# Cross-attention and FFN on one core: the prologue in another order, loads over both queues, scores ahead of VW

## The chip, the cores and the metric

One core of a Trainium2 chip runs the whole program. The metric is the device time of one execution in microseconds (us). TensorE is called PE, VectorE DVE, ScalarE ACT, GpSimd POOL and SyncE SP, as in the profile.

## The reference, cut to what matters

x is 2 x 1024 x 256, the context 2 x 77 x 192, all fp32.

```python
x = x + xattn(layernorm(x), ctx, Wq, Wk, Wv, Wo, bo)   # 8 heads of 64
x = x + ffn(layernorm(x), gamma, beta, ...)
# xattn: softmax((h @ Wq) (ctx @ Wk)^T * 64**-0.5) @ (ctx @ Wv) @ Wo + bo
# ffn:   h = layernorm(x) * gamma + beta; w = (q - 128) * scales (fc1: 256 x 1024, fc2: 1024 x 256)
#        x + 0.5 * (silu(h @ w1 + b1) @ w2 + b2)
```

## The kernel before

**What is computed.** x is worked on in eight pairs (a = 0 to 7) of two tiles of 128 rows; pairs 0 to 3 are batch 0, 4 to 7 batch 1. Since the context is short, keys and queries are folded once for each batch b: M = Wq K^T (256 x 616, called M{b}.{n}: n // 2 is the half of the 256 rows, n % 2 the even or the odd heads) and VW = V Wo (616 x 256, VW{b}.0 to .2). For a pair the work is then: transposes of x (XT), scores (S{a}.{j}: x M), the maximum over each head subtracted (DVE), exp with the row's rstd as scale (ACT), sums and reciprocals (DVE), normalize (POOL), transposes of the probabilities (PT), attention_out (AO: probabilities times VW, with bo as one more row of VW), the second layer norm (hn), its transposes (HT), fc1 in four parts (F1.{a}.{p}), silu (ACT), fc2 (F2.{a}.{j}), the sum and the store. Every matmul operand in fp32 is split into a high and a low part, and three products are added: the high part is a copy by ACT (DVE for h), the low part a subtraction, by DVE for x, M, VW, probabilities, h and w2, by POOL for w1 and y.

**What sets the order.** Nothing is scheduled: each engine's block is a list of calls, and that list is the order in which it works. Engines wait for each other by semaphores. PSUM is six buffers (S0 and S1 of two banks, H0, H1, T0, T1 of one). The list `order` (line 62) says which result takes which buffer after which: a result can be written when its predecessor in the same buffer has been freed, and each buffer counts how often it was filled and freed.

**The places that the change touches.** SP's and ACT's blocks begin with the loads (lines 223 to 235, 353 to 358); SP then waits until VW0.2 is free and writes bo's two halves into the bias rows (238 to 241), and only behind that issues q2, s2 and the x pairs 3 to 7 (242 to 245); the bias rows of batch 1 follow when VW1.2 is free. POOL (323 to 349): rsqrt1 (rstd of the first layer norm, which exp needs), dequantize_w1, normalize, lower_w1, rsqrt2 (the roots of the second one: one for each tile that hn needs, then the residual's), lower_y, add_b2. DVE from 638, ACT from 445, PE from 856. On PE, `scores` waits for all four parts of M where a % 4 = 0 (796), `attention_out` for VW and the bias rows of its batch (816 to 819), again only where a % 4 = 0. From pair 2 on each engine runs a loop (499, 692, 916; POOL from pair 1, 337).

Of the kernel before, what the change touches and what calls it, by code (L numbers as in the profile page):

```python
# [13 lines left out]
P = 128  # L14
# [11 lines left out]
def build_program(nc, x, ctx_in, wq, wk, wv, wo, bo, gamma, beta, q1, s1, b1, q2, s2, b2, out):  # L26
# [39 lines left out]
    for a in range(1, NA):  # L66
        if a > 1:
            order += [(f"S{a}.0", "S0"), (f"S{a}.1", "S1"), (f"F2.{a - 2}.1", "T1"), (f"HT{a - 1}", "S0")]
        order += [(f"F1.{a - 1}.{p}", f"H{1 - p % 2}") for p in range(HP)]
        order += [(f"PT{a}.0", "S1"), (f"PT{a}.1", "S0"), (f"AO{a}.0", "T0"), (f"AO{a}.1", "T1")]  # L70
        order += [(f"XT{a + 1}", "S1")] * (a < LAST) + [(f"F2.{a - 1}.0", "T0")]
# [8 lines left out]
    with ExitStack() as stack:  # L80
# [45 lines left out]
        table_probe = small("table_probe", [P, 1])  # L126
# [66 lines left out]
        bo_hi_done, bo_split = sem("bo_hi_done"), sem("bo_split")  # L193
# [25 lines left out]
        with nc.Block() as block:  # L219

            @block.sync
            def _(sp):
                sp.dma_start(ctx_sb[:, :, :], ctx_v).then_inc(ctx_in_sem, 16)
                sp.dma_start(wq_sb[:, :, :], wq.rearrange("(n p) f -> p n f", p=P)).then_inc(wq_in, 16)
# [33 lines left out]
            def _(pool):  # L258
# [54 lines left out]
                def dequantize_w1(n):  # L313
                    c, cols = n // 2, slice(n % 2 * F // 2, (n % 2 + 1) * F // 2)
# [3 lines left out]
                def lower_w1(n):  # L318
                    c, cols = n // 2, slice(n % 2 * F // 2, (n % 2 + 1) * F // 2)
# [5 lines left out]
                nc.gpsimd.tensor_scalar(b2_half[:, :], b2_half[:, :], 0.5, None, ALU.mult).then_inc(b2_done, 1)  # L325
                pool.wait_ge(s1_in, 16 * C)
                for n in range(2 * C - 1):
                    dequantize_w1(n)
                normalize(0, 0)
                normalize(0, 1)  # L330
                dequantize_w1(2 * C - 1)
                for n in range(2 * C):
                    lower_w1(n)
                rsqrt1(1)
                rsqrt2(0)
                pool.wait_ge(b2_done, 1)
                for a in range(1, NA):
# [6 lines left out]
                    rsqrt2(a)  # L344
# [7 lines left out]
            def _(act):  # L352
                act.dma_start(wk_sb[:, :, :], wk.rearrange("(n p) f -> p n f", p=CC)).then_inc(wk_in, 16)
                act.dma_start(x_sb[:, pair(0), :], x_v[:, pair(0), :]).then_inc(x_in[0], 16)
                act.wait_ge(half_ready, 1)
                nc.scalar.activation(table_probe[:, :], neg_half[:, 0:1], ACT.Exp)
# [78 lines left out]

                def shift_w1(n):
                    c, cols = n // 2, slice(n % 2 * F // 2, (n % 2 + 1) * F // 2)
                    nc.scalar.activation(w1_sb[:, c, cols], q1_sb[:, c, cols], ACT.Copy, bias=-ZERO_POINT).then_inc(w1_shifted, 1)

                def split_w1(n):  # L440
                    c, cols = n // 2, slice(n % 2 * F // 2, (n % 2 + 1) * F // 2)
# [48 lines left out]
                for n in range(2):  # L490
                    half = slice(n * M // 2, (n + 1) * M // 2)
                    act.wait_ge(w2_done, n + 1)
                    nc.scalar.activation(w2_hi[:, half, :], w2_sb[:, half, :], ACT.Copy).then_inc(w2_hi_done, 1)
# [484 lines left out]
```

## Time and profile before

| | |
|---|---|
| three runs, median (lowest, highest) | 189.31 us (188.37, 191.15) |
| the profiled execution | 188.6 us |
| its span, first to last instruction | 186.8 us |
| busy share of the span: PE, DVE, ACT, POOL | 97%, 66%, 66%, 62% |
| granted clock of PE, mean | 0.998 |
| DMA | 10.72 MB, mostly in the first 28 us |

The page has a line of tenths for each engine (40 slices of 4.7 us). PE is at 9 from about slice 11 to the end but for the last; DVE has its fullest stretch, 9 or close to it, in slices 4 to 11 (14 to 51 us), which is the prologue. Ends of matmuls are modelled and overlap the next one, so where PE waits is read from the distances between starts, not from its busy time.

### The profile page before, as it was taken

What the parts mean: (1) busy time and instruction counts of PE and PEld (TensorE: products, weight loads), DVE (VectorE), ACT (ScalarE), POOL (GpSimd) and SP (SyncE); (2) the same over time, 40 slices, a digit from 0 to 9 for tenths busy, and PEclk for the clock granted to TensorE, in tenths of its full rate; (3) what the DMA queues carried; (4) which work ended last, traced back from release to release, by engine and by line L of the source; (5) the groups of instructions that cost most, each with busy time, mean ns of one, the idle gap of its engine ahead of it and who ended that gap; (6) DMA issues with size and microseconds to landing.
All of it is one profiled execution on the core that took longest, in us unless ns stands there. A gap on an engine that the chain in (4) does not pass through costs nothing.

```text
span 186.8 us, 3886 instructions
## 1 busy us (share of the span) xinstructions
PE 180.7 (97%) x1502; PEld 177.0 (95%) x1502; DVE 122.4 (66%) x261; ACT 122.5 (66%) x230; POOL 116.2 (62%) x159
## 2 busy tenths in 40 slices
PE   7999899899899999999999999999999999999994
PEld 7999699689899999999999999999999999999994
DVE  0287988899969464964496557937594768255341
ACT  3287880599918981898368944896289817962580
POOL 5032998569983977099707972597439762776220
PEclk9999999999999999999999999999999999999999
DMA  6997990000000100010001000100001000100101
GB/s 171 325 399 185 357 353 13 2 0 4 2 0 0 60 0 0 4 56 0 4 0 56 4 0 0 33 30 0 0 4 56 0 4 0 56 4 0 56 4 56
DMA packets 9480, 10.72 MB, mean 57 GB/s; under 512 B 2268, under 2 KB 8183, under 8 KB 9335
## 3 DMA queue, kind: packets, MB, share of 16 engines
q1 hardware_dynamic: 8837, 9.70, 15.7%
q10 hardware_dynamic: 626, 0.79, 1.5%
q8 instruction: 12, 0.20, 0.4%
q14 instruction: 5, 0.04, 0.1%
HBM read 8.38 MB, written 2.10 MB: 56 GB/s over the span
## 4 chain that ended last, share of the span: by engine, by line
PE 78%; DVE 9%; POOL 9%; ACT 1%; issue 1%
PE T L852 22%; PE H L838 21%; PE T L823 11%; PE S L802 11%; PE S L809 4%; PE S L755 3%; POOL q_sb L316 3%; POOL w_lo L321 3%; PE S L733 2%; DVE w_lo L631 2%; POOL probs L279 1%; DVE q_sb L625 1%; PE T L740 1%; PE H L740 1%; POOL rstd L290 1%
## 5 line engine op out<-in xcount | busy, mean ns | idle before, releaser
L311 POOL TENSOR_TENSOR y_lo<-y,y_hi 128x512 fp32r<-128x512 f32 x28 | 37.6, 1363 | 2.1 <-ACT y_hi L434 1.6
L279 POOL TENSOR_TENSOR probs<-probs,rsum 128x616 f32<-128x616 f32 x16 | 19.1, 1218 | 31.4 <-DVE rsum L583 31.4
L852 PE MATMUL T<-w_hi,y_hi 128*128 128x256 f32 x128 | 36.7, 286 | 0.6 <-DVE x_sb L594 0.6
L838 PE MATMUL H<-hT_hi,w_hi 128*128 128x256 f32 x128 | 36.7, 287 | 0.1
L838 PE MATMUL H<-hT_lo,w_hi 128*128 128x256 f32 x128 | 35.5, 277 | 0.0
L838 PE MATMUL H<-hT_hi,w_lo 128*128 128x256 f32 x128 | 35.5, 277 | 0.0
L852 PE MATMUL T<-w_lo,y_hi 128*128 128x256 f32 x128 | 35.5, 277 | 0.0
L852 PE MATMUL T<-w_hi,y_lo 128*128 128x256 f32 x128 | 35.4, 277 | 0.0
L430 ACT ACTIVATE y<-H,vec 128x256 f32<-128x256 f32 x64 | 26.5, 467 | 6.6 <-PE H L838 6.6
L403 ACT ACTIVATE probs<-probs,rstd 128x616 f32<-128x616 f32 x16 | 12.9, 807 | 27.1 <-DVE probs L571 27.1
L588 DVE TENSOR_TENSOR pT_lo<-S,pT_hi 128x640 fp32r<-128x640 f32 x16 | 13.1, 823 | 18.1 <-ACT pT_hi L407 18.1
L852 PEld LDWEIGHTS T<-w_hi,y_hi 128*128 128x128 f32 x128 | 24.1, 188 | 0.9 <-DVE x_sb L594 0.9
L838 PEld LDWEIGHTS H<-hT_hi,w_hi 128*128 128x128 f32 x128 | 24.1, 188 | 0.5 <-issue 0.5
L852 PEld LDWEIGHTS T<-w_lo,y_hi 128*128 128x128 f32 x128 | 24.1, 189 | 0.0
L838 PEld LDWEIGHTS H<-hT_lo,w_hi 128*128 128x128 f32 x128 | 24.1, 188 | 0.0
L852 PEld LDWEIGHTS T<-w_hi,y_lo 128*128 128x128 f32 x128 | 24.1, 188 | 0.0
L838 PEld LDWEIGHTS H<-hT_hi,w_lo 128*128 128x128 f32 x128 | 24.1, 188 | 0.0
L823 PE MATMUL T<-vw_hi,pT_hi 128*128 128x256 f32 x80 | 22.4, 280 | 0.0
L823 PE MATMUL T<-vw_lo,pT_hi 128*128 128x256 f32 x80 | 22.1, 277 | 0.0
L823 PE MATMUL T<-vw_hi,pT_lo 128*128 128x256 f32 x80 | 22.1, 277 | 0.0
L434 ACT ACTIVATE y_hi<-y 128x512 fp32r<-128x512 f32 x32 | 20.2, 632 | 1.0
L564 DVE TENSOR_REDUCE smax<-S 128x8 f32<-128x616 f32 x16 | 12.8, 799 | 12.0 <-PE S L802 11.5
(127 smaller groups left out, 460.6 us busy)
## 6 DMA issues: line engine op xcount, KB each, us to landing
q_sb<-in_L_ffn_fc_q SPq DMA_DIRECT2D x2, 1024.0 KB, 8.0
out_x<-x_sb SPq DMA_DIRECT2D x16, 128.0 KB, 1.8
x_sb<-in_x SPq DMA_DIRECT2D x7, 256.0 KB, 8.2
s_sb<-in_L_ffn_fc_scales SPq DMA_DIRECT2D x2, 512.0 KB, 12.0
s_sb<-in_L_ffn_fc_scales SPq DMA_DIRECT2D x1, 1024.0 KB, 7.7
wq_sb<-in_L_xattn_Wq SPq DMA_DIRECT2D x1, 512.0 KB, 5.6
wo_sb<-in_L_xattn_Wo SPq DMA_DIRECT2D x1, 512.0 KB, 8.1
wk_sb<-in_L_xattn_Wk ACTq DMA_DIRECT2D x1, 384.0 KB, 4.1
```

The source lines that it names most:

```text
L279: nc.gpsimd.tensor_tensor(p, p, rsum[:, j, :].unsqueeze(2).to_broadcast([P, HEADS, J]), ALU.mult).then_inc(norm_done, 1)
L311: nc.gpsimd.tensor_tensor(y_lo[:, two, :], y[:, two, :], f32(y_hi[:, two, :]), ALU.subtract).then_inc(y_lo_done, 1)
L403: nc.scalar.activation(probs[:, j, 0:HJ], probs[:, j, 0:HJ], ACT.Exp, scale=rstd1[:, t:t + 1]).then_inc(exp_done, 1)
L430: ins = nc.scalar.activation(y[:, m, :], r[:, q * W:(q + 1) * W], ACT.Silu, bias=b1_sb[:, m:m + 1])
L434: nc.scalar.activation(y_hi[:, two, :], y[:, two, :], ACT.Copy).then_inc(y_hi_done, 1)
L564: nc.vector.tensor_reduce(smax[:, j, :].rearrange("p (n h) -> p n h", n=2), s, AX_X, ALU.max).then_inc(max_done, 1)
L588: nc.vector.tensor_tensor(flat(pT_lo[:, j, :, :]), ps[bank][:, 0:JC * P], flat(f32(pT_hi[:, j, :, :])), ALU.subtract).then_inc(freed[bank], 1)
L802: ins = mm(o, xt[:, c, j * P:(j + 1) * P], m[:, b, c, h, 0:HALF], start=n == 0, stop=n == len(steps) - 1)
L809: ins = nc.tensor.transpose(r[:, m * P:(m + 1) * P], probs[:, j, m * P:(m + 1) * P], ident[:, :])
L823: ins = mm(r[:, 0:D], p[:, j, m, :], v[:, b * JC + m, :], start=n == 0, stop=n == len(steps) - 1)
L838: ins = mm(r[:, q * W:(q + 1) * W], wt[:, c, m * P:(m + 1) * P], ht[:, c, :], start=c == q == i == 0, stop=c == q == 1 and i == 2)
L852: ins = mm(o, yt[:, m, j * P:(j + 1) * P], wt[:, m, :], start=m == 0 and i == 0, stop=m == M - 1 and i == 2)
```

## The change

- **Loads.** Wk is loaded in halves of 96 rows, one on ACT's queue, one on SP's behind ctx and ahead of Wq; `wk_in` is awaited at 32.
- **PE.** Five warm matmuls at the start instead of eight. scores(0, .) stands right behind M0, ahead of the three VW0. M1.0 stays near the first probabilities, M1.1 goes behind VW1.2, just ahead of fc1(0, 0). fc1(0, 2) goes between the two prob_transposes of pair 1, x_transposes(2) ahead of attention_out(1, .), and fc2(0, 0) behind scores(2, .).
- **Finer waits.** scores(0, 0) waits for the even parts of M before its first half, for the odd ones before its second (new semaphore m_even_done). The bias rows are awaited ahead of the last chunk of attention_out, not at its start. w1 is split by column halves first (c = n % 2), so that fc1(0, 0) and (0, 1) wait for two of four quarters, fc1(0, 2) for all.
- **POOL.** It takes over bo's split. normalize(0, .) stands behind one dequantize_w1 instead of three. rsqrt2 is split in root2 (for hn) and residual_roots; the root2 of pair 0 stand ahead of rsqrt1(1) and of the last two lower_w1. In pair 1 rsqrt1(2) stands behind two lower_y, and root2(1, .) ahead of the last.
- **ACT and DVE** follow PE's order; make_hn(0) is parted around score_maxima(1, 0); the w2_hi parts and lower_w2 are parted, and lower_w2(1) goes behind add_attention(1, 1). residual(0) goes into the first round of the loop, ahead of scale_h(1).
- **Place list.** S0.0 and S0.1 swap buffers, M1.2 and M1.3 share S0.

```diff
-             ("M0.0", "H1"), ("M0.1", "T0"), ("M0.23", "S0"), ("VW0.2", "T1"), ("VW0.0", "H0"), ("S0.0", "S0"), ("S0.1", "S1"),
+             ("M0.0", "H1"), ("M0.1", "T0"), ("M0.23", "S0"), ("S0.0", "S1"), ("S0.1", "S0"), ("VW0.2", "T1"), ("VW0.0", "H0"), ("VW0.1", "T0"),
...
+                sp.dma_start(wk_sb[:, 1, :], wk[CC:DC, :]).then_inc(wk_in, 16)
                 sp.dma_start(wq_sb[:, :, :], wq.rearrange("(n p) f -> p n f", p=P)).then_inc(wq_in, 16)
...
-                act.dma_start(wk_sb[:, :, :], wk.rearrange("(n p) f -> p n f", p=CC)).then_inc(wk_in, 16)
+                act.dma_start(wk_sb[:, 0, :], wk[0:CC, :]).then_inc(wk_in, 16)
...
                     for h in range(2):
+                        if j == 0 and a % AB == 0:
+
+                            wait_freed(pe, m_home(b, h)[0])
+                            if h == 0:
+                                pe.wait_ge(m_even_done, b + 1)
+                            else:
+                                wait_freed(pe, m_home(b, 3)[0])
...
-                warm(8)
+                warm(5)
...
                 for c in range(C):
                     make_m(0, c)
+                scores(0, 0)
+                scores(0, 1)
                 pe.wait_ge(wo_in, 16)
...
                 make_vw(0, 2)
                 make_vw(0, 0)
-                scores(0, 0)
-                scores(0, 1)
                 make_vw(0, 1)
                 x_transposes(1)
-                make_m(1, 0)
                 pe.wait_ge(probs_ready, 1)
                 prob_transposes(0, 0)
-                make_m(1, 1)
+                make_m(1, 0)
                 prob_transposes(0, 1)
...
                 make_vw(1, 1)
                 make_vw(1, 2)
-                pe.wait_ge(w1_split, 2 * C)
+                make_m(1, 1)
                 fc1(0, 0)
                 fc1(0, 1)
                 prob_transposes(1, 0)
+                fc1(0, 2)
                 prob_transposes(1, 1)
-                fc1(0, 2)
                 fc1(0, 3)
+                x_transposes(2)
                 attention_out(1, 0)
                 attention_out(1, 1)
-                x_transposes(2)
-                fc2(0, 0)
                 for a in range(2, LAST):
                     scores(a, 0)
                     scores(a, 1)
+                    if a == 2:
+                        fc2(0, 0)
                     fc2(a - 2, 1, range(1))
```

PE behind M of batch 0, before (kT and wqT make M, wo_sb and vT VW, m and xT scores):

```order
L774 MATMUL S<-kT,wqT 128x77 x8
L786 MATMUL T<-wo_sb,vT 128x256
L786 MATMUL H<-wo_sb,vT 128x256 x3
L802 MATMUL S<-m_hi,xT_hi 128x308
L802 MATMUL S<-m_lo,xT_hi 128x308
```

and in the changed kernel:

```order
L799 MATMUL S<-kT,wqT 128x77 x8
L834 MATMUL S<-m_hi,xT_hi 128x308
L834 MATMUL S<-m_lo,xT_hi 128x308
...
L813 MATMUL T<-wo_sb,vT 128x256
L813 MATMUL H<-wo_sb,vT 128x256 x3
L813 MATMUL T<-wo_sb,vT 128x256 x4
L780 MATMUL S<-ident,x_sb 128x128 x4
L841 MATMUL S<-ident,probs 128x128 x5
```

Scores now follow M with nothing between them, and the three VW stand together behind.

POOL around the first normalize (probs<-probs,rsum), before:

```order
L316 TENSOR_TENSOR q_sb<-q_sb,s_sb 128x512 x3
L279 TENSOR_TENSOR probs<-probs,rsum 128x616 x2
L316 TENSOR_TENSOR q_sb<-q_sb,s_sb 128x512
L321 TENSOR_TENSOR w_lo<-q_sb,w_hi 128x512 x4
L272 TENSOR_SCALAR veps<-mv 128x2
L274 TENSOR_TENSOR rstd<-veps,neg_half 128x2
L287 TENSOR_SCALAR vars<-mv 128x1
L290 TENSOR_TENSOR rstd<-vars,neg_half 128x1
```

and in the changed kernel:

```order
L319 TENSOR_TENSOR q_sb<-q_sb,s_sb 128x512
L280 TENSOR_TENSOR probs<-probs,rsum 128x616 x2
L319 TENSOR_TENSOR q_sb<-q_sb,s_sb 128x512
L324 TENSOR_TENSOR w_lo<-q_sb,w_hi 128x512 x2
L319 TENSOR_TENSOR q_sb<-q_sb,s_sb 128x512 x2
L287 TENSOR_SCALAR vars<-mv 128x1
L290 TENSOR_TENSOR rstd<-vars,neg_half 128x1
```

One dequantize stands ahead of normalize, and two lower_w1 have moved behind the roots.

DVE between pair 1's reciprocals and the h of pair 1 (q_sb<-q_sb,s_sb dequantizes w2), in the changed kernel:

```order
L571 SCALAR_TENSOR_TENSOR m_lo<-S,m_hi 128x308 x2
L651 SCALAR_TENSOR_TENSOR q_sb<-q_sb,s_sb 128x1024 x2
L614 TENSOR_TENSOR pT_lo<-S,pT_hi 128x640
L579 TENSOR_TENSOR vw_lo<-T,vw_hi 128x512
...
L585 TENSOR_TENSOR xT_lo<-S,xT_hi 128x512
L657 TENSOR_TENSOR w_lo<-q_sb,w_hi 128x1024
L620 TENSOR_TENSOR x_sb<-T,x_sb 128x256
...
L657 TENSOR_TENSOR w_lo<-q_sb,w_hi 128x1024
L630 SCALAR_TENSOR_TENSOR hn<-x_sb,mv,rstd 128x256 x2
```

Before, the two vw_lo and the statistics stood ahead of the dequantization, no m_lo stood here, both lower_w2 (w_lo) stood ahead of the additions of attention (x_sb<-T,x_sb), and the low part of x pair 2 (xT_lo) behind them.

## Rows read from the trace of the kernel before

**Rows 1.** The page, engines: busy us (share of the span) xinstructions
```profile
PE 180.7 (97%) x1502; PEld 177.0 (95%) x1502; DVE 122.4 (66%) x261; ACT 122.5 (66%) x230; POOL 116.2 (62%) x159
```

**Rows 2.** Windows, core 0: stretch, its length, busy us (xinstructions), clock, DMA share, GB/s
```profile
5.80:11.40 5.60, 5.60 (x44) 5.53 (x44) 2.30 (x6) 2.84 (x7) 0.23 (x1) 1.00 1.08 343
...
0.00:58.40 58.40, 54.89 (x426) 51.66 (x427) 44.34 (x89) 37.21 (x72) 38.43 (x52) 1.00 0.45 145
58.40:187.00 128.60, 125.78 (x1078) 125.38 (x1076) 78.10 (x174) 85.31 (x159) 77.81 (x107) 1.00 0.05 18
```

**Rows 3.** Timeline of PE: start us, us, engine, line, operation [idle before <-releaser]
```profile
12.44 1.06 PE L774 MATMUL S<-kT,wqT 64*128 64x77 f32 x16
...
15.12 0.44 PE L802 MATMUL S<-m_hi,xT_hi 128*128 128x308 f32 x1
...
20.61 0.63 PE L755 MATMUL S<-ident,x_sb 128*128 128x128 f32 x4
...
22.79 0.74 PE L809 MATMUL S<-ident,probs 128*128 128x128 f32 x5 [0.51 <-issue]
...
24.51 0.77 PE L809 MATMUL S<-ident,probs 128*128 128x128 f32 x5
...
33.89 0.66 PE L755 MATMUL H<-ident,hn 128*128 128x128 f32 x4 [0.53 <-DVE hn L604]
...
34.38 2.33 PE L786 MATMUL T<-wo_sb,vT 128*128 128x256 f32 x10
...
36.84 0.36 PE L838 MATMUL H<-hT_hi,w_hi 128*128 128x256 f32 x1
...
40.94 0.77 PE L809 MATMUL S<-ident,probs 128*128 128x128 f32 x5 [0.41 <-POOL probs L279]
...
49.02 0.38 PE L852 MATMUL T<-w_hi,y_hi 128*128 128x256 f32 x1 [0.65 <-DVE x_sb L594]
```

**Rows 4.** The chain that ended last: start us, us, what
```profile
1.03 3.78 PE S L733 x16
...
21.48 2.39 POOL probs L279 x2
...
25.11 4.99 POOL w_lo L321 x4
```

**Rows 5.** By source line, L733: ns min/median/max, first and last start
```profile
L733 PE MATMUL S<-warm_sb x18: 275/422/580, 1.0 to 5.4; 128*128 128x128 f32 x18
```

**Rows 6.** DMA issues: queue, operation xcount, KB each, us from issue to landing
```profile
wq_sb<-in_L_xattn_Wq SPq DMA_DIRECT2D x1, 512.0 KB, 5.6
...
wk_sb<-in_L_xattn_Wk ACTq DMA_DIRECT2D x1, 384.0 KB, 4.1
```

**Rows 7.** Timeline of DVE, columns as in rows 3
```profile
14.01 0.86 DVE L544 SCALAR_TENSOR_TENSOR m_lo<-S,m_hi 128x308 fp32r<-128x308 f32 x2
...
17.14 0.80 DVE L564 TENSOR_REDUCE smax<-S 128x8 f32<-128x616 f32 x1 [0.36 <-PE S L802]
...
21.19 0.20 DVE L583 RECIPROCAL rsum<-ssum 128x8 f32<-128x8 f32 x1
...
39.04 0.20 DVE L583 RECIPROCAL rsum<-ssum 128x8 f32<-128x8 f32 x1
...
54.60 0.80 DVE L571 TENSOR_TENSOR probs<-S,smax 128x616 f32<-128x616 f32 x1
```

**Rows 8.** Timeline of POOL and ACT, as in rows 3; last row by source line
```profile
17.65 3.78 POOL L316 TENSOR_TENSOR q_sb<-q_sb,s_sb 128x512 f32<-128x512 f32 x3 [4.48 <-ACT q_sb L438]
...
42.50 1.55 POOL L274 TENSOR_TENSOR rstd<-veps,neg_half 128x2 f32<-128x2 f32 x1
...
62.35 0.71 POOL L274 TENSOR_TENSOR rstd<-veps,neg_half 128x2 f32<-128x2 f32 x1
...
69.53 1.08 ACT L420 ACTIVATE x_sb<-x_sb,res_shift,res_scale 128x256 f32<-128x256 f32 x2
...
L631 DVE TENSOR_TENSOR w_lo<-q_sb,w_hi x2: 1542/1927/2312, 44.9 to 46.3; 128x1024 fp32r<-128x1024 f32 x2
```

More of the change, by code:

```diff
@@ L325, in _ @@
                 nc.gpsimd.tensor_scalar(b2_half[:, :], b2_half[:, :], 0.5, None, ALU.mult).then_inc(b2_done, 1)
+                pool.wait_ge(bo_in, 16)
+                nc.gpsimd.tensor_copy(bo_hi[:, :], bo_sb[:, :]).then_inc(bo_hi_done, 1)
+                pool.wait_ge(bo_hi_done, 1)
+                nc.gpsimd.tensor_tensor(bo_lo[:, :], bo_sb[:, :], f32(bo_hi[:, :]), ALU.subtract).then_inc(bo_split, 1)
                 pool.wait_ge(s1_in, 16 * C)
-                for n in range(2 * C - 1):
-                    dequantize_w1(n)
+                dequantize_w1(0)
                 normalize(0, 0)
                 normalize(0, 1)
-                dequantize_w1(2 * C - 1)
-                for n in range(2 * C):
-                    lower_w1(n)
+                dequantize_w1(1)
+                lower_w1(0)
+                lower_w1(1)
+                dequantize_w1(2)
+                dequantize_w1(3)
+                root2(0, 0)
+                root2(0, 1)
                 rsqrt1(1)
-                rsqrt2(0)
+                lower_w1(2)
+                lower_w1(3)
+                residual_roots(0)
                 pool.wait_ge(b2_done, 1)
-                for a in range(1, NA):
+                normalize(1, 0)
+                normalize(1, 1)
+                lower_y(0, 0)
+                lower_y(0, 1)
+                rsqrt1(2)
+                lower_y(0, 2)
+                root2(1, 0)
+                root2(1, 1)
+                lower_y(0, 3)
+                residual_roots(1)
+                add_b2(0)
+                for a in range(2, NA):
                     normalize(a, 0)
@@ L488, in _ @@
                 prob_hi(1, 0)
+                vw_hi_part(1, 1)
                 prob_hi(1, 1)
[L490 to L493, printed above, removed]
+                vw_hi_part(1, 2)
+                x_hi(2)
+                w2_hi_part(0)
                 hidden(0, 2)
+                w2_hi_part(1)
                 hidden(0, 3)
[L496 to L498 removed]
+                nc.scalar.activation(table_probe[:, 0:1], neg_half[:, 0:1], ACT.Exp)
                 for a in range(2, NA):
                     exponential(a, 0)
+                    if a == 2:
+                        residual(0)
                     scale_h(a - 1)
                     exponential(a, 1)
[L503 removed]
+                    nc.scalar.activation(table_probe[:, 1:2], neg_half[:, 0:1], ACT.Silu)
                     hidden(a - 1, 0)
@@ L545, in m_lo_part @@
                                                          f32(m_heads(m_hi, b, n)), ALU.mult, ALU.subtract)
-                    if (b, n) != (0, 2):
-                        ins.then_inc(freed[bank], 1)
+                    ins.then_inc(m_even_done if n == 2 else freed[bank], 1)
                 def vw_lo_part(b, n):
@@ L684, in _ @@
                 prob_lo(1, 0)
+                vw_lo_part(1, 1)
+                stats1(2)
                 prob_lo(1, 1)
+                vw_lo_part(1, 2)
+                x_lo(2)
                 lower_w2(0)
-                lower_w2(1)
                 add_attention(1, 0)
                 add_attention(1, 1)
-                x_lo(2)
+                lower_w2(1)
                 make_hn(1)
@@ L777, in make_m, with make_vw @@
                             fill(homes[e][0], ins[e])
-                def make_vw(b, n):
-                    r = emptied(f"VW{b}.{n}")
-                    for q in range(min(2, JC - 2 * n)):
+                def make_vw(b, n, qs=range(2)):
+                    if qs[0] == 0:
+                        emptied(f"VW{b}.{n}")
+                    r = ps[place[f"VW{b}.{n}"][0]]
+                    for q in qs[:JC - 2 * n]:
                         m = 2 * n + q
```

121 lines of the change are left out of this document (59 added, 62 removed), and 4 rows, old and new, of the table order.

## The prediction

> **What bounds the kernel now.** I read the page first: TensorE (PE) is busy for 97% of the 186.8 us span [rows 1]. The windows view then splits the span. From 58.4 us on, which the change leaves as it is, PE is busy 125.8 of 128.6 us (what is missing lies at the very end, in work that is not touched); what can be removed lies in the prologue, 0 to 58.4 us [rows 2]. A busy PE there hides work that merely follows other work, so I went by the starts of PE's stages. In PE's timeline [rows 3] six stages don't start right behind the last record ahead of them: the transposes of x pair 1 (20.61), of the first probabilities (22.79), of hn (33.89), fc1 (36.84), the second probabilities of pair 1 (40.94) and fc2 (49.02). Beyond the usual 0.12 from start to start these are about 0.35, 0.65, 0.7, 0.4, 0.55 and 0.8 us, 3.5 us together. (The idle time that the rows print is counted from a modelled end and is smaller.) Who ends them: POOL, which in the chain of work holds everything from 21.48 on with normalize and the split of w1 [rows 4], then DVE with hn and x_sb [rows 3]. So at most 3.5 us, plus what the start gives, is to be had: 2% of the span. The rest is matmuls that are neither added nor removed.
>
> **The change, stage by stage.** I carry the start of each PE stage forward, each with the durations of the rows. "Now" is the kernel before.
>
> *Start.* Three warm matmuls go: six records; 16 take 3.78 us with the modelled tail of the last [rows 4], a new one each 0.21, so 1.28 us. What follows waits for ctx. When that lands the views don't say; wk, issued at the same time on the other queue, took 4.1 us, to about 4.8 [rows 6]. So the gain is between 0 and 1.28; the transposes of ctx now stand directly behind the last warm record, and I take 0.2, near the lower end. K then starts behind the two copies of ctxT, not behind wk, so halving wk over two queues earns nothing. It puts 192 KB more ahead of wq on SP's queue. wq landed at 1.20 + 5.6 = 6.8 and is wanted at 7.85 [rows 6]; at the 343 GB/s of that stretch [rows 2] 192 KB is up to 0.6 us, and x's first tiles lose as much on the other queue. It stays hidden: cost 0, 0 to 0.3 if not. M's last half (16 records from 12.44 [rows 3]) now ends at 13.4, in the new order 13.2.
>
> *Scores ahead of VW.* Eight records of VW, 1.7 us between M and scores at 15.12, are gone from there. But scores needs the low parts of M, the even one for its first half: DVE makes them from 14.01 for 0.86 us, two in a row [rows 7], so the first is there at 14.45, 14.25 with the earlier start. Scores starts at 14.35 instead of 15.12. PE idles about 1.1 us, where it had VW: this is a new wait. Then 3.4 us of scores (24 records) and 3.4 of the three VW (16 records, 0.21 each as in the ten from 34.38) bring the x transposes to 21.15 (20.61 now).
>
> *First probabilities.* The DVE chain from smax (17.14) to the end of the reciprocal (21.19 + 0.2) [rows 7] moves 0.77 earlier, to 20.6. POOL does one dequantize (1.26, of 3.78 for three, from 17.65 on) ahead of normalize, not three, and is free [rows 4, 8]; the two operations on bo that it takes over lie in its 4.48 us of idle time ahead of the dequantize and cost nothing (if not, 1.2 each at most, as one of 128x512). Normalize takes 1.2 (2.39 for two), so the transposes start at 22.0 (22.79 now); PE waits 0.4. The second pair: rsum waits for a vw_lo of 0.41, to 22.0; normalize to 23.2; x_lo, which frees the bank, to 23.3; transposes at 23.6 (24.51 now [rows 3]). One M is no longer in front of them. From there VW, attention and scores run closed for 8.7 us as now (33.9 less the wait of 0.7, less 24.5), to 32.3.
>
> *hn.* POOL's queue after normalize is re-dealt: one dequantize, two lower_w1 with a wait of about 0.65 for ACT's copy ahead of the second, two more dequantize (5 x 1.26 + 0.65 behind 23.2, to 30.15), then the roots that hn needs (0.85 each; the second wants mv at 30.2) to 31.9, hn 0.48 behind smax, to 32.7. Transposes of h at 32.8 (33.89 now), PE waits 0.5.
>
> *fc1.* VW 2.05 (ten records), and the M that was moved here, 0.95 (16 records) [rows 3]: fc1 starts at 36.4 (36.84 now). split_h would be ready at 35.7: the moved M fills the 0.4 us wait that stood here. fc1 needs only half of w1 split, 27.6. POOL ends the rest of w1 at 35.4 and the residual roots at 37.5, so normalize of pair 1 runs 37.6 to 40.0. PE: transposes 39.3, fc1 39.9, second transposes 41.3 (0.55 wait gone, because fc1(0,2) lies between), fc1 and x transposes to 43.8, attention 43.85 to 47.3. Now attention starts at 44.28 and still has the x transposes (0.45) behind it: 0.9 us ahead. Its banks are freed by vw_lo at 43.0 and 45.2; the bias rows of batch 1 are first waited for at pair 4. Those of batch 0 are issued when vw_lo ends (21.2 instead of 15.5), and q2, s2 and five x pairs are queued behind them, 5.7 us later, from about 22.7; q2 and s2, 1 MB each, are 6 us at 343 GB/s, and DVE wants them at 39, so 0.
>
> *fc2 behind scores.* The 0.8 us for which fc2(0,0) waited on DVE [rows 3] is covered by scores: scores at 47.35, fc2 50.8 to 53.6, then 3 records. Transposes of h 1 could start at 54.0 (55.59 now). DVE is next: from its last reciprocal (39.04 + 0.2) to the end of the subtraction that frees the bank (54.60 + 0.8) it takes 16.2 us, 1.5 of it the two waits for POOL's roots [rows 7]. In the new order it starts 0.75 earlier, carries two m_lo (0.86) more and has the second lower_w2 over one or both waits: 38.5 + 0.85 + 14.7 = 54.05. So 54.15. Last, residual(0) (1.08 [rows 8]) now stands in ACT ahead of scale_h(1): exp 0.8, residual 1.08, scale 0.5, split 0.75 behind 54.05 give fc1(1,0) at 57.25, against 58.43 now: 1.2 us ahead. The residual also delays DVE's ssum, so POOL's normalize(2,0) ends at about 60.1 where PE wants it at 59.97: 0.2 back.
>
> *POOL beside DVE.* While DVE dequantizes w2, POOL's small root operation takes 1.55 us at 42.50, and 0.71 at 62.35 [rows 8]. The new order puts normalize(1,1) there (39.05 on). If it is stretched alike it ends at 41.4 and PE waits 0.1; two-sided bound 0 to 1. I take 0. The Trainium skill (GPSIMD Engine Reference, Specifications) says why: POOL shares its SBUF interfaces with VectorE when that reads two SBUF inputs. The rows agree; by its rule the loss sits at this place.
>
> Sum: 0.2 (start) + 0.6 (scores earlier, 14.35 for 15.12 less the start) are what the softmax chain gets; carried through, 1.2 us at fc1(1,0), less 0.2: **1.0 us**. The profiled execution took 188.6 us (span 186.8 and 1.8 around it): 187.6. The three runs shown have 189.31 as median, 0.7 above it, and 188.37 as lowest; I add 0.2 for that: **187.8**.
>
> **Rivals.**
> (a) *Clock.* Warm records at the start take 422 ns, the last one, at 5.4, takes 275 [rows 5]. So PE starts at the lower of its levels (1.2 GHz) and gets 2.4 GHz around 5.3, after 4.3 us of matmuls almost without a pause. With five warm matmuls PE pauses from 3.2 until ctx lands, up to 1.1 us. If only the work behind the pause counts, the rise comes at 4.2 + 4.3 = 8.5: 3.1 us at half speed, a loss of 1.55, and 187.8 becomes 189.3, slower than before. It decides as soon as the rise comes over 2 us later, that is after 7.3. For it: nothing else changes in that stretch. Against it: the pause is a quarter of it at most. The Trainium skill (TensorE: Matmul & The Clock Gate, Part 1) tells that the default state is throttled and activity releases it, which is this rival's rule; this trace has no pause to try it on. 15%.
> (b) *Nothing arrives.* The 1.1 us wait for M, DVE's chain and residual(0) in ACT give back the rest; each term of 0.1 to 0.4 is as large as my error in a hand-off. 187.8 + 1.0 = 188.8. 17%.
> (c) *More arrives.* ctx is there by 3.5 (another 0.6), and hn or DVE's queue is not late (0.5 + 0.3): 187.8 - 1.4 = 186.4; all waits gone would be 188.6 - 3.5 - 0.2 = 184.9. 13%.
> (d) *DVE late.* With lower_w2 at 2.31 rather than 1.54 us each beside POOL's lower_y [rows 8], fc2's second half and hn come up to 1.5 later: 187.8 + 1.5 = 189.3. 5%.
> Forecast, a gain of 0.4 to 1.8: 50%.
>
> **Numbers.** Leaving out the far ends of (a) and (c), 185.9 to 189.5 holds 8 in 10. Faster by over 2% (about what a measurement of this kernel can tell from no change) is below 185.5: only the far end of (c) with a low draw of runs, 8%. Slower by over 2% is above 193.1, beyond every rival: 3%. Within 2%: 89%.
>
> **What would show it.** PE: ctx transposes 0.2 earlier; a gap of about 1.1 ahead of scores; probability transposes at 22.0; h transposes at 32.8; no gap at fc1, at the second transposes of pair 1 or at fc2; fc1(1,0) at 57.2. A PE record of 422 ns behind 5.8 speaks for (a). A gap ahead of the h transposes at 54, or of fc2's middle, speaks for (d). I am wrong if ctx is late, if wq is, or if hand-offs between engines (0.05 to 0.15 each in the rows) are longer in the new order.

## The result, and the profile after

The changed kernel takes 193.7 us (median of 4; 193.59 to 194.71) against 189.11 us before (4; 188.37 to 191.15): a ratio of 1.0243, with a 95% interval of 1.0188 to 1.0297. It is slower by 4.6 us, where 187.8 us was forecast, 1.3 us below this median of before, and the time lies outside the range of 185.9 to 189.5. Here and below, a ratio leaves out the few slow executions, more than 1.5% above the fastest of their kernel, while a median is of all. The profiled execution took 193.6 us, its span is 191.8 us.

The page's engine line and the first line of the chain of work that ended last (shares of the span by engine), to be read beside [rows 1]:

```profile
PE 182.9 (95%) x1496; PEld 178.5 (93%) x1496; DVE 125.1 (65%) x260; ACT 122.7 (64%) x229; POOL 117.4 (61%) x161
...
PE 78%; DVE 11%; POOL 3%; ACT 2%; DMA 2%; issue 1%
```

PE is busy 2.2 us longer (180.7 before) though it has six matmuls fewer: some of them ran slower. The rest of the 5.0 us by which the span has grown is waiting. The waits view of PE lists what it waited for (us in total, times, longest; "PE S L780 <- DVE pT_lo L614" is a transpose at line 780 into buffer S that waited for DVE's operation at line 614):

```profile
PE S L780 <- DVE pT_lo L614: 1.2, 1, 1.2
PE S L834 <- DVE m_lo L571: 1.1, 1, 1.1
PE T L899 <- DMA ctx_sb<-in_ctx: 1.1, 1, 1.1
...
PE H L874 <- DVE hT_lo L639: 0.7, 1, 0.7
PE H L780 <- DVE hn L630: 0.4, 1, 0.4
...
PE T L856 <- DVE vw_lo L579: 0.2, 1, 0.2
```

m_lo and ctx were foreseen. pT_lo (ahead of the transposes of x pair 2), hT_lo (ahead of fc1(1,0)) and vw_lo (ahead of the second half of attention) were not. The windows view, cut at the starts of M, of the first transposes of h (HT) and of fc1(1,0), first of before and then of after (columns as in [rows 2]), tells how much each stretch lost (the fourth row of after is the rest of the span):

```profile
0.00:11.49 11.49, 10.31 (x66) 9.97 (x67) 2.78 (x8) 4.69 (x10) 2.99 (x12) 1.00 0.90 275
11.49:33.89 22.40, 21.27 (x179) 19.50 (x179) 19.20 (x41) 13.38 (x28) 17.21 (x19) 1.00 0.70 235
33.89:58.43 24.54, 23.35 (x183) 22.22 (x184) 22.39 (x41) 19.17 (x34) 18.23 (x23) 1.00 0.01 1
```

```profile
0.00:14.09 14.09, 11.94 (x61) 11.26 (x61) 2.78 (x8) 4.73 (x11) 3.03 (x12) 1.00 0.85 264
14.09:35.83 21.74, 20.07 (x164) 18.63 (x163) 18.00 (x38) 12.57 (x25) 14.94 (x17) 1.00 0.63 209
35.83:63.25 27.42, 24.91 (x199) 23.17 (x199) 25.71 (x41) 19.95 (x36) 21.04 (x27) 1.00 0.03 8
63.25:191.80 128.55, 125.94 (x1076) 125.44 (x1076) 78.62 (x175) 85.44 (x159) 78.42 (x107) 1.00 0.05 18
```

The start lost 2.60 us, the stretch from M to HT gained 0.66, the one from HT to fc1(1,0) lost 2.88, of which 0.95 is M1.1, moved there out of the stretch ahead. Leaving M1.1 out, the first stretch lost 0.29 and the second 1.93. Behind 63.25 us nothing has changed (128.55 against 128.37).

**The start.** PE's timeline of after:

```profile
1.04 2.50 PE L758 MATMUL S<-warm_sb 128*128 128x128 f32 x10 [1.04 <-DVE warm_sb L664]
4.66 0.46 PE L899 MATMUL T<-ident,ctx_sb 77*96 77x77 f32 x2 [1.11 <-DMA ctx_sb<-in_ctx]
...
5.85 2.39 PE L765 MATMUL T<-ctxT,wk_sb 96*128 96x154 f32 x8
8.03 2.26 PE L765 MATMUL H<-ctxT,wk_sb 96*128 96x154 f32 x8
10.09 1.06 PE L773 MATMUL H<-ident,wq_sb 128*128 128x128 f32 x4
...
11.46 0.60 PE L780 MATMUL S<-ident,x_sb 128*128 128x128 f32 x4
11.89 1.22 PE L765 MATMUL T<-ctxT,wv_sb 96*128 96x154 f32 x8
```

K starts at 5.85 us (5.80 before), but its 16 records take until 10.09, 4.24 us, and the same shape takes 2.20 us for V behind 11.89. The windows print a granted clock of 1.00 here, so the level has to be read from the records, which start 0.27 us apart in K and 0.14 in V: K runs at 1.2 GHz, and from about 11 us on PE runs at 2.4 GHz. M starts 2.60 us late, and 2.55 of them are lost between K and the transposes of x.

**Behind HT.** DVE's timeline of after:

```profile
37.94 1.35 DVE L637 CAST hT_hi<-hT 128x256 fp32r<-128x256 f32 x1
...
39.66 0.28 DVE L637 CAST hT_hi<-hT 128x256 fp32r<-128x256 f32 x1
...
42.89 4.31 DVE L651 SCALAR_TENSOR_TENSOR q_sb<-q_sb,s_sb 128x1024 f32<-128x1024 int32 x2
...
56.34 1.50 DVE L630 SCALAR_TENSOR_TENSOR hn<-x_sb,mv,rstd 128x256 f32<-128x256 f32 x1 [0.45 <-POOL rstd L290]
...
61.70 1.04 DVE L637 CAST hT_hi<-hT 128x256 fp32r<-128x256 f32 x1 [0.78 <-ACT hT L437]
```

and POOL's over the same time:

```profile
36.62 2.51 POOL L324 TENSOR_TENSOR w_lo<-q_sb,w_hi 128x512 fp32r<-128x512 f32 x2
...
41.50 2.39 POOL L280 TENSOR_TENSOR probs<-probs,rsum 128x616 f32<-128x616 f32 x2 [0.40 <-DVE rsum L609]
43.85 4.48 POOL L314 TENSOR_TENSOR y_lo<-y,y_hi 128x512 fp32r<-128x512 f32 x2
...
61.29 1.29 POOL L308 TENSOR_TENSOR x_sb<-x_sb,b_half 128x512 f32<-128x512 f32 x1 [1.80 <-ACT x_sb L445]
```

The two dequantize_w2 take 4.31 us on DVE. Before, they took 2.35 at 41.13 us, beside two small operations of POOL, of which the second ends at 44.05 [rows 8]; now normalize and two lower_y run beside them, and the lower_y take 2.24 us each, where one otherwise takes 1.28. The first cast of hT_hi takes 1.35 us beside POOL's lower_w1, the second 0.28 without it. Three rows show the form of it: the cast of 37.94 ends at 39.29, 0.16 us behind the lower_w1 that ends at 39.13; the cast of 61.70 ends at 62.74, 0.16 behind the add_b2 that ends at 62.58; and the second hn of pair 1, 1.50 us where the first takes 0.48, ends at 57.84, 0.28 behind a lower_y (56.27, 1.29 us). The three POOL operations take no longer than elsewhere (1.26, 1.29 and 1.29 us). So DVE seems to be held until POOL's operation is over, rather than to run at a lower rate; beside the dequantization POOL's lower_y are held as well. This reading is an inference from the ends of the rows. The collision isn't new: in the kernel before it fell on the two lower_w2 (3.78 us for the pair, 1.22 and 1.19 in after), which stood behind the low parts of the probabilities, and PE waited 0.6 us for x_sb behind them. In the changed kernel POOL's lower_y start earlier beside DVE's list and fall on the dequantization, ahead of these low parts, and there PE waits 1.2 us.

### The profile page after: what moved, and what is told of

Read it like the earlier page. It is cut to its first block, busy times and chain, and to the rows that moved or that the text cites. A ratio compares the mean times of both kernels' runs of the same rounds, so it can differ in the third digit from the quotient of the medians.

```text
span 191.8 us, 3874 instructions
## 1 busy us (share of the span) xinstructions
PE 182.9 (95%) x1496; PEld 178.5 (93%) x1496; DVE 125.1 (65%) x260; ACT 122.7 (64%) x229; POOL 117.4 (61%) x161
## 4 chain that ended last, share of the span: by engine, by line
PE 78%; DVE 11%; POOL 3%; ACT 2%; DMA 2%; issue 1%
PE H L874 20%; PE T L888 19%; PE T L856 12%; PE S L834 11%; PE S L841 4%; PE S L780 3%; DVE q_sb L651 2%; DMA ctx_sb<-in_ctx 2%; PE T L765 2%; PE H L765 2%; DVE hn L630 2%; PE H L813 1%; DVE hT_hi L637 1%; POOL rstd L290 1%; DVE probs L597 1%
## 5 line engine op out<-in xcount | busy, mean ns | idle before, releaser
L314 POOL TENSOR_TENSOR y_lo<-y,y_hi 128x512 fp32r<-128x512 f32 x28 | 38.1, 1382 | 3.1 <-ACT y_hi L459 2.7
L614 DVE TENSOR_TENSOR pT_lo<-S,pT_hi 128x640 fp32r<-128x640 f32 x16 | 13.1, 822 | 17.8 <-ACT pT_hi L432 17.8
```

The lines of the kernel that those rows point to most:

```text
L314: nc.gpsimd.tensor_tensor(y_lo[:, two, :], y[:, two, :], f32(y_hi[:, two, :]), ALU.subtract).then_inc(y_lo_done, 1)
L614: nc.vector.tensor_tensor(flat(pT_lo[:, j, :, :]), ps[bank][:, 0:JC * P], flat(f32(pT_hi[:, j, :, :])), ALU.subtract).then_inc(freed[bank], 1)
```

## The experiments

All times are medians of the executions of a kernel. The kernel before had 189.10 us beside e1 to e4, 189.15 beside f1 to f4, 188.92 beside g2 and g3, and 189.07 beside h1. The last three columns are lengths in the profile of each: from 0 to M, from M to HT, and from HT to fc1(1,0). They show where; the medians show how much. Four of the profiled executions are not typical of their kernel: those of e1 (194.8 us), g2 (190.0) and g3 (190.4) took about 2 us more than the median, that of e2 (189.9) 1.4 us less, so their column "to M" is not that of the median.

| kernel | median us (lowest, highest; n) | ratio to before | to M | M to HT | HT to fc1(1,0) |
|---|---|---|---|---|---|
| before | 189.1 | | 11.49 | 22.40 | 24.54 |
| after | 193.7 (193.59, 194.71; 4) | 1.0243 [1.0188, 1.0297] | 14.09 | 21.74 | 27.42 |
| e1 | 192.6 (192.09, 194.78; 5) | 1.0147 [1.0075, 1.0218] | 13.78 | 23.28 | 27.40 |
| e2 | 191.3 (189.89, 192.04; 10) | 1.0086 [1.0044, 1.0128] | 12.83 | 22.41 | 24.53 |
| e3 | 189.8 (189.01, 190.11; 10) | 1.0025 [0.9995, 1.0054] | 12.74 | 22.41 | 24.54 |
| e4 | 191.4 (191.15, 193.89; 4) | 1.0125 [1.0040, 1.0210] | 12.94 | 21.73 | 26.55 |
| f1 | 190.3 (189.70, 192.29; 10) | 1.0075 [1.0038, 1.0111] | 11.97 | 21.74 | 26.56 |
| f2 | 189.6 (189.34, 192.91; 10) | 1.0022 [0.9988, 1.0057] | 11.89 | 21.74 | 25.58 |
| f3 | 189.6 (189.26, 193.22; 10) | 1.0012 [0.9972, 1.0053] | 11.65 | 22.89 | 24.61 |
| f4 | 189.2 (188.98, 192.99; 10) | 0.9997 [0.9971, 1.0023] | 11.87 | 21.73 | 25.47 |
| g2 | 188.0 (187.75, 189.99; 13) | 0.9945 [0.9917, 0.9973] | 13.80 | 20.87 | 25.18 |
| g3 | 188.4 (187.81, 190.36; 12) | 0.9963 [0.9923, 1.0002] | 13.86 | 20.98 | 25.41 |
| h1 | 188.6 (187.77, 189.03; 12) | 0.9965 [0.9938, 0.9992] | 12.84 | 20.87 | 25.17 |

### The start: e1, e2, e3

Theory: fewer warm matmuls make the clock rise late, and halving wk delays later loads. Rival: the start costs little, and the loss is in the new order. First the changed kernel with eight warm matmuls (e1):

```diff
-                warm(5)
+                warm(8)
```

> The changed kernel with eight warm matmuls instead of five. Theory P (the pause behind the warm matmuls holds PE at the lower clock until 10.7 us): K runs at 0.13 us a record again, M starts at 11.3 to 11.6 instead of 14.1 and the time falls by 2.2 to 2.8, to about 191.1. Rival D (wk in two halves and later landings delay the start, the clock rises at random): M stays at 13 or later and the time at 193 to 194.

Measured: 192.6 us, 1.1 less than the changed kernel: neither the 2.2 to 2.8 of theory P nor the 193 to 194 of rival D. In its profile, which is of an execution 2.2 us above the median, the clock is late again: K's first eight records take 2.39 us, as in after, though PE has no pause ahead of the transposes of ctx (4.66 us, right behind the 16 warm records). So a late rise doesn't need the pause. Next the kernel before with five (e2, the same edit the other way round):

> The kernel before with five warm matmuls and nothing else changed. Theory P: records of 0.26 us in K, M at about 14, the time up by 2 to 2.8, to 191.1 to 191.9. Rival D: 189.1, within 0.5 of before.

Measured: 191.3 us, 2.2 more than before, or 1.6 by the ratio. PE's timeline of e2:

```profile
3.59 0.47 PE L863 MATMUL T<-ident,ctx_sb 77*96 77x77 f32 x2
...
5.04 2.42 PE L740 MATMUL T<-ctxT,wk_sb 96*128 96x154 f32 x8 [0.22 <-DMA wk_sb<-in_L_xattn_Wk]
7.26 2.23 PE L740 MATMUL H<-ctxT,wk_sb 96*128 96x154 f32 x8
9.31 0.61 PE L748 MATMUL H<-ident,wq_sb 128*128 128x128 f32 x4
```

ctx is there at 3.59 us, with hardly a pause, K starts 0.76 us earlier than before, and M 1.34 later, because K runs at the lower level. This is the fastest of the ten executions; the others lie at 190.4 to 192.0, which no profile shows. One edit costs the kernel before 1.6 to 2.2 us, which bears out theory P's time though not its pause. Then the kernel before with wk in halves (e3):

```diff
+                sp.dma_start(wk_sb[:, 1, :], wk[CC:DC, :]).then_inc(wk_in, 16)
...
-                act.dma_start(wk_sb[:, :, :], wk.rearrange("(n p) f -> p n f", p=CC)).then_inc(wk_in, 16)
+                act.dma_start(wk_sb[:, 0, :], wk[0:CC, :]).then_inc(wk_in, 16)
```

> The kernel before with wk in two halves over two queues, nothing else. Theory P: nothing on the path waits for wk or wq, so 189.1 within 0.5, M at 11.5. Rival D: ctx at 4.5, wq at 7.6 or later, M later by 0.3 to 2.5 and the time up by as much.

Measured: 189.8 us, 0.7 more; the interval of the ratio just includes 1, so the loss is not shown by the times of e3 alone. The clock was early in its profile, and yet M starts 1.25 us late. Its timeline, and then its DMA issues (queue, KB, us from issue to landing) show why:

```profile
8.99 0.60 PE L756 MATMUL S<-ident,x_sb 128*128 128x128 f32 x4
10.44 1.32 PE L741 MATMUL T<-ctxT,wv_sb 96*128 96x154 f32 x8 [0.85 <-DMA wv_sb<-in_L_xattn_Wv]
```

```profile
wv_sb<-in_L_xattn_Wv SPq DMA_DIRECT2D x1, 384.0 KB, 8.4
x_sb<-in_x ACTq DMA_DIRECT2D x1, 256.0 KB, 4.7
```

wv takes 8.4 us from issue to landing, against 6.8 before, and is issued 0.4 us later (2.03 against 1.65); V waits for it. x's first tiles, on ACT's queue, take 4.7 us (6.5 before). Moving 192 KB from ACT's queue to SP's has let x pass and made wq (6.2 us, 5.6 before) and wv behind it on SP's queue late. The Trainium skill (DMA: Bandwidth & Descriptors, Issuing engines are not separate DMA queues) says that loads of both queues end up on the same 16 DMA engines and interleave, so that a second queue saves only issue time; the trace agrees, since the bytes were shifted and not sped up.

### Down the stairs: e4, f1, f2, f4

e4 is e1 with residual(0) back outside ACT's loop, behind which scale_h(1) no longer stands.

> The changed kernel with eight warm matmuls and residual(0) back behind hidden(0, 3), outside the loop, where ACT is idle. If residual(0) ahead of scale_h(1) costs what the trace of the changed kernel suggests (PE waits 0.97 at fc1(1, 0), POOL's add_b2 stretches hT_hi from 0.28 to 1.04), the time is 0.8 to 1.5 below that with eight warm matmuls alone, near 190. Rival: DVE's queue is the limit there anyway, and the difference is under 0.3.

Measured: 191.4 us, 1.2 less than e1, and fc1(1,0) follows without a wait. The hT_hi cast is back at 0.28 us. The edit takes away two things at once, scale_h(1)'s place behind residual(0) and add_b2 beside the cast, and no run parts them. The 1.2 is within the forecast difference of 0.8 to 1.5; the time itself, near 190, was missed. Its clock was early, and V waited 1.2 us for wv. f1 is e4 with wk in one piece:

> The kernel of e4 (changed kernel, eight warm matmuls, residual(0) outside the loop) with wk loaded in one piece on ACT's queue, as before. Theory W (two halves put wv behind more bytes: it landed at 10.4 to 10.8 in all four traces with halves, at 8.5 to 8.7 without, and PE waits 1.1 to 1.4 at V): M starts at 11.5 instead of 12.9, 1.2 to 1.4 less than e4, 190.1. Rival: the landings differ from run to run for another reason, and the time stays at 191.2 to 191.5.

Measured: 190.3 us, another 1.2 less, as theory W has it; the ratio falls from 1.0125 to 1.0075. Undoing the warm matmuls gained 1.1 (after to e1), undoing wk as well another 1.2: in after the late clock puts M at 14.09 us, and a late wv alone would put it at 12.9 (e4), so V doesn't wait for wv as long as the clock is late. The halves alone were not undone in the changed kernel; by these rows that should gain little. f2 and f4 then test whether DVE is slow because POOL works beside it. f2 puts the second dequantize_w2 (and the statistics of x pair 2) further back; f4 leaves DVE alone and holds POOL until both are done, ahead of lower_y(0,0):

```diff
+                pool.wait_ge(w2_done, 2)
```

> f1 with the second dequantize_w2 behind x_lo(2) on DVE, so that the two are apart and prob_lo(1, 0) waits for one of them. Theory C (dequantize_w2 takes 2.1 us instead of 1.2 because POOL's normalize and lower_y run beside it, and stands between the probabilities and PE): the 1.5 us wait at the transposes of x pair 2 goes, the second dequantize takes 1.2 to 1.5, and the time falls by 1 to 2 below f1, to 188.1 to 189.1. Rival: DVE is full there anyway, the wait moves to the transposes of h of pair 1 or to fc2, and the time is within 0.5 of f1.

> f1 with POOL held ahead of lower_y(0, 0) until both dequantize_w2 are done. Theory C: then only normalize lies beside them, DVE's pair of dequantize takes 3.0 to 3.6 instead of 4.3 us, and the wait at the transposes of x pair 2 shrinks by as much; the time falls by 0.3 to 1 below f1. Rival (the dequantize is slow because of its own operands): still 4.2 or more.

Measured: f2 189.6 us, 0.7 less than f1: less than theory C's 1 to 2, more than the rival's 0.5. The same operations of DVE in f1 and then in f2:

```profile
40.78 4.31 DVE L649 SCALAR_TENSOR_TENSOR q_sb<-q_sb,s_sb 128x1024 f32<-128x1024 int32 x2
```

```profile
40.70 2.08 DVE L649 SCALAR_TENSOR_TENSOR q_sb<-q_sb,s_sb 128x1024 f32<-128x1024 int32 x1
...
46.87 1.21 DVE L649 SCALAR_TENSOR_TENSOR q_sb<-q_sb,s_sb 128x1024 f32<-128x1024 int32 x1
```

The second dequantize_w2, which has only a small POOL operation beside it, takes 1.21 us, the first 2.08, and the wait at the transposes of x pair 2 is gone. But PE now waits 0.6 us ahead of the second HT (0.3 in f1) and 0.5 for a lower_y ahead of fc2's second half, which takes back a part. f4 takes 189.2 us, 1.1 less than f1, a little over the 0.3 to 1 of theory C. Here is DVE's row in f4, and then POOL's timeline:

```profile
40.67 3.21 DVE L650 SCALAR_TENSOR_TENSOR q_sb<-q_sb,s_sb 128x1024 f32<-128x1024 int32 x2
```

```profile
39.27 2.39 POOL L279 TENSOR_TENSOR probs<-probs,rsum 128x616 f32<-128x616 f32 x2 [0.39 <-DVE rsum L608]
43.95 2.54 POOL L313 TENSOR_TENSOR y_lo<-y,y_hi 128x512 fp32r<-128x512 f32 x2 [2.29 <-DVE q_sb L650]
```

Nothing was changed on DVE, and its pair takes 1.10 us less; normalize still lies beside its first 1.0 us. POOL waits 2.3 us, takes 2.54 for two lower_y (4.48 in f1), and is done at 46.49 us, 0.3 later than in f1. This shows the cause, and rules out the rival (the operation's own operands): two engines that got in each other's way lose next to nothing by taking turns.

With f4 the staircase is down at the time of before: 193.7, 192.6, 191.4, 190.3, 189.2. Three steps undo an edit; the last one takes away a collision. The steps were taken in this one order, so the size of each holds with the ones before it in place. What is left of the change then gives nothing, where 1.0 was forecast.

### What is left: f3, g2, g3, h1

f3 is the kernel before with one part of the change alone: scores(0, .) ahead of VW, with the finer waits for M that this needs.

> The kernel before with scores(0, .) alone moved ahead of VW, with the finer waits for M and the order on ACT and DVE that this needs (vw_hi and vw_lo behind exp and shift_scores); eight warm matmuls, one wk, POOL as before. By my stage walk: PE waits 1.1 to 1.4 ahead of scores, smax of pair 0 starts 0.5 to 0.8 earlier, but POOL still does three dequantize ahead of normalize, so the probability transposes stay near 22.8: 188.8 to 189.8. Rival: the new wait lets PE's clock fall in some runs (seen in the trace of e1), and the median rises by 1 or more.

Measured: 189.6 us, a ratio of 1.0012: no difference, as forecast. Its waits view shows that the waits of before have moved:

```profile
PE S L807 <- DVE m_lo L544: 1.1, 1, 1.1
...
PE T L857 <- DVE x_sb L593: 0.5, 1, 0.5
PE T L828 <- DVE m_lo L544: 0.4, 1, 0.4
PE S L814 <- POOL probs L279: 0.4, 1, 0.4
```

The 1.1 us ahead of scores are as forecast; VW, which used to cover them, stands in a place that had no wait of that size. So work that doesn't need m_lo is wanted in the gap. g2 is f4 with M1.0 there, which needs two other buffers of PSUM, and DVE casting batch 1's m_lo behind batch 0's:

```diff
                 for c in range(C):
                     make_m(0, c)
+                pe.wait_ge(v_even_done, 2)
+                make_m(1, 0)
                 scores(0, 0)
...
-                make_m(1, 0)
                 prob_transposes(0, 1)
```

> This is the kernel of f4_f1_pool_held with the first part of batch 1's M (36 products, 1.9 us) moved ahead of the scores of stage (0,0), into the 1.4 us in which TensorE waits for VectorE's m_lo casts; the casts of batch 1's M follow those of batch 0 on VectorE. My theory (the gap ahead of the scores is what the new order costs, and it is also where the granted clock can fall): TensorE's wait ahead of the scores falls from 1.40 to 0.5 us or less, no execution has a mean granted clock near 0.991, and the median is 188.4 to 188.9 (0.3 to 0.7 under f4's 189.18). Rival: what binds from the scores to HT is VectorE and GpSimd, so the 0.9 us come back as longer waits ahead of PT or HT; then the median stays at 189.0 to 189.3 and only the executions at the lower mean clock are gone.

Measured: 188.0 us, ratio 0.9945 with 0.9917 to 0.9973: half a percent faster than before, 1.2 us under f4 by the medians or 1.0 by the ratios, and below the 188.4 to 188.9 of the theory. Its waits view, whole:

```profile
PE S L757 <- DVE warm_sb L663: 1.0, 1, 1.0
PE S L840 <- DVE xT_lo L584: 0.7, 1, 0.7
PE S L779 <- DVE probs L596: 0.3, 1, 0.3
PE S L833 <- DVE m_lo L570: 0.2, 1, 0.2
PE S L779 <- DVE pT_lo L613: 0.2, 1, 0.2
```

m_lo is down to 0.2. From M to fc1(1,0) g2 takes 46.05 us, before 46.94: 0.9 less, near the 1.0 that was forecast for the change. The 0.7 for xT_lo is the second transposes of probabilities, which stand directly behind the first now that M1.0 is gone from between them, and take the buffer that the cast of x_lo frees. Even so HT comes 0.86 us earlier behind M than in f4. The second hn of pair 1 still takes 1.51 us beside a lower_y in g2, on DVE's way to the second HT: a collision that no run has taken away. g3 spreads the two dequantize_w2 as well:

> g2_m1_in_gap with the second dequantize_w2 of the first pass put behind the cast of x_lo(2) on VectorE, so that GpSimd is held back for one dequantize only. My theory: the wait ahead of XT2 is under 0.2 us (0.42 in f4_f1_pool_held), the wait ahead of the second HT grows by 0.2 to 0.4, and the median is within 0.2 of g2_m1_in_gap, 188.2 to 188.9. Rival: the work of VectorE between the second scores and the second HT is the bound, so that its median is 0.3 or more above g2's.

Measured: 188.4 us. It is 0.4 above g2, on the rival's side (0.3 or more), with the wait ahead of the second HT 0.3 longer and a new one of 0.7 us for a lower_y at fc2; the intervals of the two ratios overlap, so only that it brings nothing is safe. h1 asks once more about the clock, since g2's profile had a late rise (10.3 us) with eight warm matmuls: eleven instead.

> g2_m1_in_gap with eleven warm matmuls at the start (22 records) in place of eight (16). In g2's profile the clock rose only at 10.3 us, with eight; in before's at 5.3, also with eight. Theory A (the number of warm matmuls sets when the clock rises, and late rises cost up to 2 us in some executions): the rise is at 6 us or earlier in the profile, K's records are of 292 ns, executions scatter less, and the median is 187.5 to 187.9 (0.1 to 0.5 under g2's 188.0). Rival B (the rise differs between executions whatever stands there): six more records of 0.21 or 0.14 us push the transposes of ctx from 4.7 to 5.2 or so and K behind them by about 0.4, the median is 188.2 to 188.5, and the profile's rise may still be late.

Measured: 188.6 us, 0.5 above g2 (0.4 by the ratios, whose intervals overlap), near rival B. The rise is seen at 7.2 us, and M starts at 12.84. The transposes of ctx start at 5.89 us instead of 4.84, later than I had said, since the extra records run at the lower level. On one point theory A was right: the executions scatter less, 187.8 to 189.0 us, with none near the 190 us that g2 and g3 reach. The median gains nothing by it.

## Why the prediction was wrong, point by point

To compare starts, 2.8 us are taken off those of after: its M is at 14.09, the forecast's at 11.49 - 0.2 = 11.29.

| | forecast | after | less 2.8 |
|---|---|---|---|
| scores | 14.35 | 17.23 | 14.43 |
| first, second transposes of probabilities | 22.0, 23.6 | 24.84, 26.55 | 22.04, 23.75 |
| HT | 32.8 | 35.83 | 33.03 |
| fc1 | 36.4 | 39.80 | 37.00 |
| second probabilities of pair 1 | 41.3 | 44.75 | 41.95 |
| attention of pair 1 | 43.85 | 48.68 | 45.88 |
| scores of pair 2 | 47.35 | 52.64 | 49.84 |
| second HT | 54.15 | 59.53 | 56.73 |
| fc1(1,0) | 57.25 | 63.25 | 60.45 |

- **Start: the largest error, 2.8 us.** "I take 0.2, near the lower end" was a gain; it became a loss. Two terms failed. The warm matmuls were priced by the time they take and not by what they are there for; rival (a) had the right direction, but put the rise at 8.5 us and the loss at 1.55, where the rise came at about 11 and cost 2.55. It was also given only 15%, and its argument from the pause was no evidence either way: e1 and e2 have a late rise with hardly a pause. With e2 the number of warm matmuls is shown to matter; how it does stays open. And "It stays hidden: cost 0, 0 to 0.3 if not" for halving wk looked at wq and x only, and not at wv behind them on SP's queue. It costs 1.25 to M (e3) or 1.2 at the end (e4 to f1). The size was low as well: 192 KB were priced at 0.6 us, and wv landed at 10.43 us instead of 8.45. In the changed kernel the late clock covered this loss, so it is no part of the 2.8.
- **Scores ahead of VW, first probabilities: right.** The gap is 1.1 us on m_lo (1.4 from start to start), scores within 0.1, transposes within 0.15.
- **hn: right** within 0.25.
- **fc1: 0.4 short, beyond the 0.23 at HT.** M1.1 fills most of the gap, but PE still waits 0.3 to 0.4 behind it, since the cast of hT_hi took 1.35 us beside lower_w1. "split_h would be ready at 35.7" used the undisturbed duration.
- **POOL beside DVE: wrong, 1.4 us at attention, and 0.45 more inside it.** This is the step "If it is stretched alike it ends at 41.4 and PE waits 0.1; two-sided bound 0 to 1. I take 0." It named the place and looked at one engine only: POOL's normalize wasn't stretched (2.39 us, as before), lower_y was, and DVE's dequantization went from 2.35 to 4.31. PE's loss lies outside the bound of 0 to 1. Rows of both engines under contention were in [rows 8], POOL's root operation and DVE's w_lo, and DVE's side belonged in the sum at this place. The wait then stood at x_transposes(2), which the change had moved ahead of attention; the second half of attention waited for vw_lo, behind the second pT_lo.
- **fc2 behind scores, and residual(0): half right.** fc2 has no wait. HT follows within 0.15 once the 2.5 us ahead of it are counted. That scale_h(1) stands behind residual(0) (ACT at 61.12 us) was in the sum, but not that add_b2, which POOL starts when the residual is there (61.29), falls on the cast of hT_hi (1.04 us for 0.28): from HT to fc1(1,0) it is 3.72 us, where 3.10 was forecast. The 0.2 that the forecast gave back was for another effect, normalize(2,0). Taking residual(0) out of the loop gained 1.2 us (e1 to e4).
- **Rivals.** (a) came true in its direction, with over one and a half times its price (2.55 for 1.55) and not by the pause alone. (b) did too, on top of it: with start, residual and collision mended, f4 stands at the time of before. Together they would have given 190.3, still below the measured time. I had weighed the rivals as alternatives; they were independent. Four parts of the change lose by themselves (the warm matmuls, wk in halves, POOL's order, residual(0)), and all but wk, which the late clock covers, show in its time. The 3% for slower came from that.

The sum is closed: +2.6 (start), -0.66 (M to HT), +2.88 (HT to fc1(1,0)), +0.18 behind it are the 5.0 us of the two spans.

## What to carry to other kernels

Price a warm-up by the matmuls that stand behind it at the lower clock, not by its own time, and leave it alone unless the profile can show that it is spare. When work is moved on GpSimd or VectorE, list what both do on large SBUF tiles in the same microseconds, and count a small VectorE operation that PE waits for as done only when the large one beside it is done; if two long ones collide, holding one for the other can cost next to nothing. When a load is split over two queues, follow every load behind it, not just the next one. And when a stage is moved forward past its cover, look for other work to put into the gap, as g2 does.

## What the runs showed of the hardware

- **The clock's rise varies.** With eight warm matmuls, PE's records reach 2.4 GHz by about 5.3 us in before, by 4.6 in e4 and f1, 3.9 in f4, about 6 in e3 and f3, and 6.5 in f2, but only at 10.4 in e1, 10.3 in g2 and 10.7 in g3, with nearly the same matmuls ahead; with five, at 9.3 (e2) and 11 (after), with eleven at 7.2. The Trainium skill (TensorE: Matmul & The Clock Gate, Part 1) says that the number of slow matmuls at a start differs from run to run of one kernel, and these rows agree. The times fit: the profiled executions of g2 and g3, with late rises, took 2.0 us more than the medians of these kernels, and of the 90 executions of before beside the experiments 14 took 190.6 to 191.2 us, 1.4 to 2.3 above the median, with a mean clock of 1.00; that these are late rises too is likely, and not shown. None of h1's 12 executions lies that far above its median. So one profile doesn't show what a warm-up is worth; the medians do (2.2 us for e2). What decides between an early and a late rise stays open.
- **It can fall again behind a short gap.** In e1's profile the scores behind the 1.4 us gap run at half speed for 3.4 us, and take 1.55 us longer than in after. PE's clock is 0.53 in the second row of the windows view of e1:

```profile
13.70:17.20 3.50, 2.37 (x36) 2.17 (x35) 2.84 (x7) 2.90 (x9) 2.67 (x4) 1.00 1.00 349
17.20:20.80 3.60, 3.60 (x17) 3.60 (x15) 1.06 (x2) 1.45 (x3) 1.28 (x1) 0.53 0.20 14
20.80:24.50 3.70, 3.70 (x22) 3.40 (x21) 3.18 (x6) 1.91 (x3) 0.00 (x0) 1.00 0.00 0
```

  Its mean granted clock is 0.991, and so it was in 14 of 53 executions of the seven kernels with this gap (after, e1, e4, f1 to f4), which took 1.1 to 3.9 us more than the median of the others of the same kernel. It was so in none of the 37 executions of g2, g3 and h1, whose gap is 0.5 us from start to start, nor of the 20 of e2 and e3, nor of the 90 of before (f3 has the gap and is otherwise nearly before: 3 of 10). That the gap opens the way is what this shows; that the loss always lies behind it was seen in the one profile only. One execution of f2 took 192.9 us at a mean clock of 1.00, which none of this explains.
- **VectorE and GpSimd hold each other up**, by more than I had expected: 2.35 to 4.31 us for a pair of 128x1024 operations with two SBUF inputs, 1.28 to 2.24 us for a subtraction of 128x512 on GpSimd, 0.28 to 1.35 us for a cast of 128x256. A short VectorE operation ended 0.16 to 0.28 us behind the GpSimd operation beside it in the three rows above. The Trainium skill (GPSIMD Engine Reference, Specifications) says that GpSimd shares its SBUF interfaces with VectorE, with contention where VectorE's instruction has two SBUF inputs or runs in a 2-port mode. The dequantization, with two SBUF inputs, agrees; whether the casts at 37.94 and 61.70 us, with one, run in such a mode, no run shows.
